# Row-max transfers issued by ScalarE, TensorE spinning at the start, Wk in four pieces, and new orders, in a cross-attention and feed-forward kernel

## The reference

```
z = layernorm(x)
q, k, v = z @ Wq, ctx @ Wk, ctx @ Wv            # 16 heads of 32
q, k = layernorm(q, gq, bq), layernorm(k, gk, bk)   # per head
x = x + softmax(q k^T / sqrt(32)) v @ Wo
z = layernorm(x)
s = z @ Win + bin                                # 64 columns
g = sum_h relu(s * W1[:, h] + b1[:, h]) * W2[:, h] + b2   # h of 16
x = x + g @ Wout + bout
```

## Time and profile before

| | us |
|---|---|
| median of 3 runs | 443.71 |
| the runs | 442.64 to 443.96 |
| the profiled execution | 445.51 |
| its span, first to last instruction | 443.7 |
| TensorE passes busy | 423.3 (95%) |
| TensorE weight loads busy | 287.2 (65%) |
| VectorE busy | 327.1 (74%) |
| ScalarE busy | 315.3 (71%) |
| GpSimd busy | 241.9 (55%) |

### The profile page before, as it was taken

How to read it: one execution, slowest core, us unless ns; L and a number is a source line. 1 busy time by engine, 2 the same in 40 slices (tenths; PEclk the granted TensorE clock), 3 DMA queues, 4 the chain that set the end, 5 groups by cost and what they waited for, 6 DMA issues and landing times.

```text
span 443.7 us, 7794 instructions
## 1 busy us (share of the span) xinstructions
PE 423.3 (95%) x2344; PEld 287.2 (65%) x2344; DVE 327.1 (74%) x652; ACT 315.3 (71%) x611; POOL 241.9 (55%) x326
## 2 busy tenths in 40 slices
PE   4999999999889999999999999999999999998994
PEld 2477887476557767576676757685665476556772
DVE  4888787746565999569874898479678985777765
ACT  5549768887487963899369974899559937953640
POOL 4419976586475484548156646165659036307084
PEclk9999999999999999999999999999999999999998
DMA  8662593965923339633493275705851980044005
GB/s 274 177 203 102 125 210 115 208 142 141 235 66 69 95 115 216 153 94 73 142 233 77 77 142 191 144 3 119 215 143 27 209 244 3 1 136 149 1 2 190
DMA packets 28106, 58.34 MB, mean 131 GB/s; under 512 B 8865, under 2 KB 9377, under 8 KB 24993
## 3 DMA queue, kind: packets, MB, share of 16 engines
q1 hardware_dynamic: 28064, 57.85, 50.5%
HBM read 22.18 MB, written 8.39 MB: 69 GB/s over the span
## 4 chain that ended last, share of the span: by engine, by line
PE 75%; DMA 7%; SPq 6%; POOL 3%; issue 3%; DVE 3%; ACT 1%; POOLq 1%; DVEq 0%; ACTq 0%
PE bank L2613 31%; PE bank L2619 9%; PE bank L2702 6%; PE bank L2690 6%; PE bank L2676 6%; PE bank L2705 4%; PE bank L2633 4%; PE bank L2755 3%; DMA out_dram<-x 3%; SPq L486 2%; SPq L433 2%; PE bank L2779 2%; DMA xin<-in_x_dram 2%; PE bank L2766 2%; DMA att<-in_L_xattn_Wk_dram 2%
## 5 line engine op out<-in xcount | busy, mean ns | idle before, releaser
L1074 DVE TENSOR_REDUCE mx<-bank 128x4 fp32r<-128x512 f32 x128 | 82.1, 684 | 21.9 <-PE bank L2676 21.5
L1854 ACT ACTIVATE prob<-bank 128x512 f32<-128x512 f32 x128 | 71.0, 609 | 16.6 <-PE bank L2690 10.7
L2702 PE MATMUL bank<-prob,v_kv 128*32 128x512 f32 x256 | 62.1, 599 | 0.0
L2705 PE MATMUL bank<-prob,den_sel 128*32 128x512 f32 x256 | 61.3, 599 | 0.0
L1935 ACT ACTIVATE hid<-s_in,b_col,w_col 128x256 f32<-128x256 f32 x105 | 56.8, 623 | 0.6 <-DVE s_in L1135 0.6
L2613 PE MATMUL bank<-wq_hi,zt_hi 128*128 128x512 f32 x128 | 51.5, 403 | 0.9 <-issue 0.9
L725 POOL TENSOR_TENSOR squares<-u 128x512 f32<-128x512 f32 x32 | 33.0, 1041 | 35.5 <-DVE ssq L1067 19.1
L737 POOL TENSOR_TENSOR qt_lo<-u,qt_hi 128x512 fp32r<-128x512 f32 x32 | 40.8, 1290 | 19.9 <-ACT qt_hi L1839 17.4
L2613 PE MATMUL bank<-wq_hi,zt_lo 128*128 128x512 f32 x128 | 50.6, 395 | 0.0
L2613 PE MATMUL bank<-wq_lo,zt_hi 128*128 128x512 f32 x128 | 50.6, 395 | 0.0
L1177 DVE SCALAR_TENSOR_TENSOR bank<-hid,w_col,bank 128x256 f32<-128x256 f32 x90 | 43.8, 487 | 5.1 <-ACT hid L1935 2.9
(11 more groups left out here) (175 smaller groups left out, 899.1 us busy)
## 6 DMA issues: line engine op xcount, KB each, us to landing
q_stack<-qt_hi SPq DMA_DIRECT2D x64, 256.0 KB, 4.7
xin<-in_x_dram SPq DMA_DIRECT2D x36, 256.0 KB, 4.1
q_stack<-qt_lo SPq DMA_DIRECT2D x32, 256.0 KB, 4.5
x<-in_x_dram SPq DMA_DIRECT2D x28, 256.0 KB, 3.8
out_dram<-x SPq DMA_DIRECT2D x28, 256.0 KB, 2.4
att<-in_L_xattn_Wk_dram SPq DMA_DIRECT2D x1, 1024.0 KB, 7.1
x<-in_L_xattn_Wq_dram SPq DMA_DIRECT2D x4, 256.0 KB, 7.5
hid<-in_L_xattn_Wv_dram SPq DMA_DIRECT2D x1, 1024.0 KB, 9.9
```

Source lines behind the costliest of these rows:

```text
L1074: dve.tensor_reduce(mx[:, :].rearrange("p (g i j) -> p g i j", g=G, i=HC)[:, :, 2 * half + r, j], maxs_banks[T][half][j][r][:, :].rearrang ...
L1854: act.activation(prob[:, h % PR, :], score_bank[t][h][:, :], ACT.Exp, scale=SCALE).then_inc(exp_done, 1)
L2702: pe.matmul(at_bank[t][c][rows(n), :], v_kv[kv_of(t)][:, n * HD:(n + 1) * HD], prob[:, n % PR, :], start=True, stop=True)
L2705: ins = pe.matmul(den_bank[t][rows(n + 2), :], den_sel[:, c, :], prob[:, n % PR, :], start=c == 0, stop=c == C - 1)
```

## The change

- stack_max moves from SyncE's order to ScalarE's, with the same two waits and the same eight transfers a block.
- Wk is fetched in four transfers of 256 KB with a semaphore each, and the first key projection waits for each chunk by itself.
- Before the context arrives TensorE makes five products of inv_d with itself (spin), into a bank that is written over later, and two more ahead of the first key projection. inv_d becomes the first memset of GpSimd.
- The row of ones (maximum_row) goes ahead of turned_ctx on ScalarE.
- On SyncE the load of Wout goes up to right behind stack_keys(0), stack_keys(1) goes ahead of the loads of x for block 4, those go ahead of the residual loads of block 0, and other loads and stores change places.
- The bank tables and the orders of all engines are written anew; in the lists of TensorE, VectorE, ScalarE and GpSimd calls move by a few places, with none added or left out but those above.

```diff
+BEFORE_CTX, BEFORE_KEYS = 5, 2
...
+        wk_loaded = [sem(f"wk_loaded{c}") for c in range(C)]
...
-            sp.dma_start(wk_in[:, :, :], Wk.rearrange("(c p) n -> p c n", p=P)).then_inc(wk_loaded, 16)
+            for c in range(C):
+                sp.dma_start(wk_in[:, c, :], Wk[c * P:(c + 1) * P, :]).then_inc(wk_loaded[c], 16)
...
-            def stack_max(T):
-
-                sp.wait_ge(mx_turned, T + 1)
...
                 stack_keys(0)
+                load_wout()
                 stack_q(0, 0)
...
-                stack_max(0)
                 stack_q(1, 0)
                 stack_q(1, 1)
                 stack_q(1, 2)
                 stack_q(1, 3)
+                stack_keys(1)
                 load_x(4, 0)
                 load_x(4, 1)
-                stack_max(1)
+                load_x(4, 2)
+                load_x(4, 3)
                 load_residual(0, 0)
-                stack_keys(1)
                 load_residual(0, 1)
                 load_residual(0, 2)
-                load_residual(0, 3)
-                load_wout()
-                load_x(4, 2)
                 stack_q(2, 0)
-                load_x(4, 3)
...
+            pool.memset(inv_d[:, :], 1.0 / D).then_inc(eyes, 1)
             pool.memset(ident[:, :], 0.0).then_inc(eyes, 1)
...
+            def stack_max(T):
+
+                act.wait_ge(mx_turned, T + 1)
+                if not first(T):
+                    act.wait_ge(scores_done, T * H)
+                place_of = q_stack[3 * HD:3 * HD + 1, :, :].rearrange("o (x e) (j a s) -> o a x (e j) s", x=2, j=TB, a=TB)
+                for a in range(TB):
+                    for x in range(2):
+                        act.dma_start(place_of[:, a, x].bitcast(F32),
+                                     mxt[32 * a:32 * (a + 1), 32 * x:32 * (x + 1)]).then_inc(max_stacked, 16)
...
             def part1():
+                maximum_row(0)
+                maximum_row(1)
                 turned_ctx(0)
                 turned_ctx(1)
-                maximum_row(0)
-                maximum_row(1)
                 guess1(0)
...
-            pe.wait_ge(consts, 1)
+            def spin(dst, count):
+
+                for n in range(count):
+                    pe.matmul(dst[:, 0:P], inv_d[:, :], inv_d[:, :], start=True, stop=True)
 
             def turn_ctx(b):
+                if b == 0:
+                    pe.wait_ge(eyes, 1)
+                    spin(ctx_bank[1], BEFORE_CTX)
+                    pe.wait_ge(consts, 1)
                 pe.wait_ge(ctx_loaded, 16)
...
-            def project_kv(dst, b, w, done):
+            def project_kv(dst, b, w, done, arrived=()):
                 for c in range(C):
+                    if arrived:
+                        pe.wait_ge(arrived[c], 16)
...
             def project_keys(b):
+                if b == 0:
+                    spin(key_bank[0], BEFORE_KEYS)
                 pe.wait_ge(ctx_moved, NB)
-                pe.wait_ge(wk_loaded, 16)
-                project_kv(key_bank[b], b, wk_in, kv_projected[0])
+                project_kv(key_bank[b], b, wk_in, kv_projected[0], wk_loaded)
```

More of the change, by code:

```diff
@@ L236, in build_program @@
[L236 to L239, removed]
+        den_bank = [banks[n] for n in (4, 0, 1, 2, 5, 7, 2, 7)]
+        s_bank = [banks[n] for n in (4, 4, 6, 1, 4, 4, 2, 0)]
+        rstd_bank = [banks[n] for n in (1, 5, 3, 2, 7, 2, 0, 3)]
+        sum_bank = {T: banks[n] for T, n in ((6, 2), (7, 0),)}
+        win_mean_bank = banks[5]
@@ L2949, in part3 @@
                 scores(0, 14)
+                pe.wait_ge(zt_lo_done, 14)
+                scores(0, 15)
                 pe.wait_ge(exp_done, 13)
[L2951 to L2958 removed]
+                project_q(3, 0, 0)
+                project_q(3, 0, 1)
@@ L3007, in part4 @@
+                spread(0, 2)
+                pe.wait_ge(u_done, 15)
+                spread(0, 3)
+                pe.wait_ge(exp_done, 20)
+                pe.wait_ge(att_done, 2)
+                max_scores(2, 0, 0)
+                project_q(3, 3, 0)
+                pe.wait_ge(att_done, 4)
+                scores(1, 4)
+                scores(1, 5)
                 pe.wait_ge(qf_done, 12)
                 pe.wait_ge(qt_hi_done, 12)
-                scores(1, 5)
-                pe.wait_ge(att_done, 3)
@@ L3135, in part6 @@
+                scores(2, 5)
+                pe.wait_ge(exp_done, 35)
+                pe.wait_ge(zt_lo_done, 20)
                 values(2, 0)
                 values(2, 1)
+                pe.wait_ge(exp_done, 37)
+                project_q(4, 3, 0)
+                pe.wait_ge(mx_done[0], 28)
+                max_scores(3, 0, 2)
+                project_q(4, 3, 1)
+                pe.wait_ge(mx_done[0], 29)
+                scores(2, 6)
+                pe.wait_ge(exp_done, 38)
+                scores(2, 7)
@@ L3137, in part6, with part7 @@
+                pe.wait_ge(att_moved, 9)
+                project_o(1, 0, 0)
+                pe.wait_ge(mx_done[0], 30)
+                values(2, 2)
+                values(2, 3)
                 pe.wait_ge(g_done, 1)
-                pe.wait_ge(att_done, 8)
+                pe.wait_ge(exp_done, 40)
                 project_y(0, 0)
-                pe.wait_ge(exp_done, 38)
+            def part7():
+                pe.wait_ge(u_done, 19)
                 project_y(0, 1)
                 pe.wait_ge(u_done, 20)
-                scores(2, 7)
@@ new lines, in part8 @@
+                spread(2, 3)
+                pe.wait_ge(mx_done[0], 36)
+                project_q(5, 3, 0)
+                pe.wait_ge(att_done, 10)
+                pe.wait_ge(u_done, 23)
+                max_scores(4, 1, 1)
+                pe.wait_ge(att_done, 11)
+                scores(3, 2)
+                project_q(5, 3, 1)
+                pe.wait_ge(exp_done, 49)
+                scores(3, 3)
+                pe.wait_ge(mx_done[1], 35)
+                scores(3, 4)
+                pe.wait_ge(exp_done, 50)
@@ new lines, in part9 @@
+                turn_q(5, 0)
+                pe.wait_ge(exp_done, 61)
+                scores(3, 14)
+                pe.wait_ge(exp_done, 62)
+                scores(3, 15)
+                pe.wait_ge(att_moved, 14)
+                max_scores(4, 0, 2)
+                project_o(2, 3, 1)
+                pe.wait_ge(att_moved, 15)
+                pe.wait_ge(mx_done[0], 37)
+                max_scores(4, 0, 3)
+                pe.wait_ge(mx_done[0], 38)
+                turn_z2(2, 0)
+                pe.wait_ge(exp_done, 64)
@@ L3391, in part10 @@
+                turn_z1(6, 3)
+                pe.wait_ge(att_done, 15)
+                max_scores(5, 1, 0)
+                pe.wait_ge(rstd_moved, 3)
+                project_q(6, 2, 0)
+                pe.wait_ge(mx_done[1], 41)
+                scores(4, 0)
+                pe.wait_ge(mx_done[1], 42)
+                pe.wait_ge(u_done, 26)
+                max_scores(5, 0, 2)
+                scores(4, 1)
+                pe.wait_ge(zt_lo_done, 28)
                 scores(4, 2)
-                pe.wait_ge(u_done, 27)
@@ L3456, in part11 @@
+                scores(4, 14)
+                pe.wait_ge(mx_done[1], 48)
+                scores(4, 15)
+                project_o(3, 2, 1)
+                pe.wait_ge(exp_done, 80)
+                project_o(3, 3, 0)
+                project_o(3, 3, 1)
+                pe.wait_ge(x1_done, 15)
+                turn_z1(7, 1)
+                pe.wait_ge(zt_lo_done, 29)
+                turn_z2(3, 0)
+                turn_z2(3, 1)
                 pe.wait_ge(x1_done, 16)
-                turn_z2(3, 0)
@@ L3637, in part14 @@
+                pe.wait_ge(att_done, 24)
+                scores(6, 6)
+                pe.wait_ge(att_moved, 25)
+                scores(6, 7)
+                pe.wait_ge(exp_done, 101)
+                scores(6, 8)
+                pe.wait_ge(mx_done[0], 59)
+                pe.wait_ge(exp_done, 102)
+                max_scores(7, 0, 2)
+                pe.wait_ge(exp_done, 103)
+                values(6, 2)
                 pe.wait_ge(mx_done[0], 60)
-                scores(6, 5)
-                scores(6, 6)
```

2184 lines of the change are left out of this document (1048 added, 1136 removed), and 32 rows, old and new, of tables (maxs_rows, score_bank).

## The result

The changed kernel is slower: 448.85 us median (446.92 to 450.45, four runs) against 443.83 of the kernel before on the same chip, a ratio of 1.0108 with a 95% interval of 1.0062 to 1.0153. Run again beside the later experiments it took 446.64 against 442.77 (1.0086, 1.0061 to 1.0110). Forecast were 441.6 and a range of 438.0 to 447.5; the time lies past the upper end of that range, 1.85 us above the first rival's 447.0, on the other side of the kernel before. The profiled execution took 447.77 us, of which 446.0 is span.

What follows compares the result with a forecast made beforehand. TensorE, busy 423.3 of 443.7 us, was taken as the bound. From the 443.71 median, start minus 1.3, SyncE's queue minus 1.8, ScalarE's holds plus 1.0 and new orders at nothing gave 441.6 us, range 438.0 to 447.5.

Steps and rivals of the forecast that it cites:

- the first rival: ScalarE becomes the bound, first in 54 to 100 us: a quarter of 40 us uncovered, 447.0 us; chance 0.24.
- ScalarE's queue: Maxima transfers in ScalarE's order hold it 5.0 us a block, 40 us in all, 4% uncovered: plus 1.0 us.
- my 0.64 per us: TensorE's assumed loss per uncovered us of ScalarE, from the wait at 108.89 us: 2.19 us cost TensorE 1.40.
- The argument for 4%: Maxima issues took the same 5 us on SyncE while TensorE was full in 154 to 208 us, so work covers them.
- SyncE's queue, minus 1.8: Second batch's keys and x of block 4 go out earlier, removing TensorE waits near 112 and 123 us; bounds 0 and 2.61.
- My list: The signs to check afterwards, among them TensorE above 53 us busy in 100 to 154 us.
- The start, minus 1.3: Spins and Wk in pieces bring keys and the fast clock earlier, limited by VectorE's slack; bounds 0.4 and 2.0 us.
- keys 0.4 us earlier: At the start, Wk in four pieces lets key passes begin at 8.0 instead of 8.41 us.
- the other reading: Counting 1.3 us at the start, with an earlier fast clock, against the skill's rule, which would count only 0.4.
- the 1.8 us against the start: Three more Wk issues of 0.59 us on SyncE could delay x and normalisation by up to 1.8 us; taken as nothing.
- Orders anew: New orders and banks on all engines, costed at nothing, with minus 1.4 to plus 1.5 us left open.
- 12% uncovered: Share of ScalarE's 40 us of holds, costing 3.1 us, from which ScalarE as the bound decides the result.

Runs made afterwards that it cites:

- both edits: Changed kernel with block 0's eight maxima transfers on SyncE and four instead of eight on ScalarE from block 1 on, part of the computation left out: 439.65 us, ratio 0.9916.
- the maxima alone: Kernel before in its own orders, with only the eight blocks' row-maxima transfers issued by ScalarE instead of SyncE: 488.05 us, ratio 1.0981.
- the start alone: Kernel before with only the spins, Wk in four pieces and the row of ones first on ScalarE: 443.39 us, ratio 0.9998.
- the maxima on GpSimd: Changed kernel with all eight blocks' row-maxima transfers issued by GpSimd instead of ScalarE: 450.27 us, ratio 1.0146.
- SyncE's order alone: Kernel before with only SyncE's order around block 1 changed (Wout, second batch's keys, x of block 4 earlier), maxima still on SyncE: 454.14 us, ratio 1.0225.

## Why the prediction was wrong

**ScalarE's queue is the step that failed.** I wrote plus 1.0, "40 us of holds, 4% uncovered". Three things in it were off.
- The size: 64 issues took 47 us, not 40, because I took one median for all of them and had named the longest, 1.404 us, without counting it. The median held (612 ns, 39 us for 64 of them). Eleven took 0.8 to 1.76 us, and most of these fell into blocks 0, 1 and 5 (holds of 7.65, 6.79 and 7.6 us), the first two in the stretch with the least room.
- The share: without the holds (block 0 on SyncE, half of the rest) the kernel is at 439.65 against 442.88, 3.2 us under the kernel before; with them 3.9 us over. They cost 7.1 us or more, since half of the later holds are still there. At my 0.64 per us, a price from one row, that is 11.1 us uncovered of 47, 24%. The rival had said a quarter and 447.0. TensorE's rows agree: its holes of more than 0.3 us between 25 and 400 us sum to 7.5 us in the changed kernel's second execution, to 4.8 in the kernel before and to 2.1 with both edits. That the maxima land later from ScalarE's queue is not the cause: no wait of TensorE in the changed kernel is put down to their transfers.
- The argument for 4%: "the same 5 us stood between max and scores on SyncE's queue, and TensorE was full". On SyncE the 5 us delay the scores of one block, for which TensorE has other work, and the transfers behind them; on ScalarE they delay all that is queued behind them, that other work's input included. The latency is the same, the queue behind it isn't.

I saw the sign of it: 9.28 us free in 54 to 100 us against two holds of 9.9, and the line "wrong if TensorE stands for ScalarE right behind the holds, first in 54 to 100 us". With the fullest window overdrawn on paper, the uncovered share there should have been read from that window (TensorE lost 2.5 busy us of 46 there) and not from an average over the run.

**The clock behind a hole had no term.** In the first execution the 2.64 us of standing were followed by half clock; in the run with the maxima alone seven holes were, and the mean granted clock was 0.949. I priced TensorE's clock at the start only. The second execution kept its clock through a hole of 2.52 us, and so did three more of its eleven, by their mean clock. So this is a risk of a long hole and no fixed price.

**SyncE's queue, minus 1.8: right in place, and in size if the holds are away.** Neither ScalarE's wait for the keys at 108.89 nor VectorE's for x at 120.39 came back; the same instructions in the changed kernel stand for nothing:

```profile
109.67 0.73 ACT L1899 ACTIVATE at_hi<-att 128x512 fp32r<-128x512 f32 x1
...
112.45 2.46 DVE L1036 BATCH_NORM_STATS2 bn<-xin 128x6 f32<-128x512 f32 x4
```

The window from 100 to 154 gained 1.42 us; with the holds halved it is full, 54.00, the whole 2.61 that was my upper bound. In the changed kernel 1.2 us of it were lost again behind block 1's hold. My list asked for more than 53 there; it was 52.81, short by that hold. What I missed is that the moves are worth nothing by themselves: with the maxima still on SyncE, behind the keys, they cost 10 us. Without most of the holds the kernel is 3.2 us under the kernel before, and this term and the start together were put at 3.1. No run shows the two gains apart, and half of the later holds are still in that run, so that the numbers meet is in part luck.

**The start, minus 1.3: the number came out by luck, its cause did not.** The first query projection came at 21.98, and I had said 22.2. But the key passes start no earlier (8.39 against 8.41; 8.20 on average with the new start, 7.98 with the old one), so "keys 0.4 us earlier" was wrong: the two spins ahead of them wait for the moved context, as the rows of TensorE in the changed kernel show, and cost the microsecond that the pieces of Wk had saved. The first piece had landed at 5.22 and the last at 7.72 in that trace, so without the spins the passes could have begun at 7.4.

```profile
7.38 1.22 PE L2630 MATMUL bank<-inv_d 128*128 128x128 f32 x4 [0.69 <-ACT scratch L1944]
...
8.39 1.06 PE L2644 MATMUL bank<-att,scratch 128*128 128x512 f32 x1
```

What did move is the fast level, to 11.73 on average from 13.04, but it moves by itself too: from 10.36 to 13.14 us with one and the same start, 10.93 to 14.52 with the old. The kernel before had the slowest start of the four traces with the old one, and I took it for the rule. On average the new start brings the queries 0.6 us earlier (21.86 against 22.44), less than either range is wide. The Trainium skill, TensorE: Matmul & The Clock Gate, Part 1, says just this, that the count of slow matmuls is a matter of the run and not to be fitted; the prediction quoted it, and put the sum by the other reading. These traces agree with the rule. By it the sum would have been 442.5.

Three smaller readings were off as well. At 4.58 TensorE waited for GpSimd's constants, as the row says, and not for the context, which had landed at 4.44. An issue of Wk took 0.46 us and not the 0.59 of other transfers, and x, issued later, was there earlier (its statistics start at 8.38 and not at 8.99), so the 1.8 us against the start had no ground. And 2.0 was no upper bound: the second execution reached the queries at 21.04, 2.47 us before 23.51.

A lead at the start also needn't reach the end. With the start alone it was gone by 239 us, behind a transfer that landed no earlier; the changed kernel without its start was 3.1 us slower, which the traces explain only in part.

**Orders anew, 0 with minus 1.4 to plus 1.5: not to be had as a number by itself.** The old orders with the holds take 488, the new with the maxima on SyncE 468, at the places tried; each order fits its own queue for the maxima, and the parts taken one at a time don't add up to the change as a whole.

The point from which the first rival decided, 12% uncovered, was right as arithmetic, and its chance of 0.24 too small: the fullest window, the one to look at for the cover, already showed on paper that there was none.

## What to carry to other kernels

A transfer's issue isn't free on an engine that computes: count the issues, allow for some that take up to three times the median, and set the sum against the free time of that engine in the very window; with none left there, TensorE stood whichever of two steps the hold pushed. Ask of a moved step not what waits for its result but what is queued behind it on its new engine, and give each block's transfers to the queue that has room at that moment. A gain read from one trace of the first 20 us, while the clock is still rising, is to be taken from several.

## What the runs showed of the hardware that I hadn't expected

One issue of a 4 KB transfer took 0.59 us (median) on SyncE, 0.61 on ScalarE and 0.50 on GpSimd. On ScalarE 11 of 64 took longer, up to 1.76 us; on GpSimd the longest took 0.752. Eight of the eleven overlap an issue of SyncE (one of them for 0.2 us alone), but three overlap none, and 19 of the short ones, of at most 0.7 us, overlap SyncE's too. The Trainium skill, Perfetto Trace Analysis, DMA Instruction — HWDGE, says that such an issue's span in the profile holds a wait for a descriptor generator that two sequencers share. That would fit the eight and GpSimd's even times; for the three it doesn't account, and no run here separates the causes. Landing too took longer than on SyncE: 2.4 us median against 1.8.

A hole of TensorE of 2.64 us was followed by 3.4 us at half clock in one execution, one of 2.52 us in another of the same kernel was not. In other runs a hole of 1.85 us (the start alone) and one of 1.97 us (the maxima on GpSimd) were followed by it too, and one of 1.99 us (SyncE's order alone) was not: among these the length of the hole doesn't tell which.
